# TensorE's loop of a four-layer kernel with two steps a turn: six turns in place of twelve

## The chip, the cores and the metric

The kernel runs on one core of one Trainium2 chip. The metric is the device time of one launch in microseconds. A core has five engines that run their own instruction streams and meet through semaphores: TensorE (PE, with its weight loads shown apart as PEld), VectorE (DVE), ScalarE (ACT), GpSimd (POOL), and SyncE (SP), which issues DMAs.

## The reference, cut to what matters

The input x is 64 sequences of 64 tokens with 512 features, float32. Four layers are applied, each added to its input:

```
x = x + x @ W.T + (x @ A[a].T) @ Bm[a].T * scal[a]   # layer 0, adapter a chosen for each sequence
x = x + w1[idx1].T @ x        # layer 1, 64x64 matrix over the tokens of each sequence
x = x + attention(x)          # layer 2, 16 heads of 32, causal, Wq, Wk, Wv, Wo
x = x + w3[idx3].T @ x        # layer 3, as layer 1 with another table
```

Large products are taken as three products of rounded parts (high by high, high by low, low by high), so one 128x128 block of a weight matrix costs three matmuls. The small products (scores, attention times values, layers 1 and 3, adapters) are float32 matmuls.

## The kernel before, in words

Four sequences (256 tokens) are worked on together and called a pair; there are 16 pairs (`PAIRS`). The kernel is a software pipeline in which step `i` works on several pairs at once: values, transposed probabilities and attention of pair `i`, layers 0 and 1 and keys, queries and scores of pair `i+1`, adapters of pair `i+2`, the output projection and layer 3 of pair `i-1`.

Each engine has its own `step(i)`, whose order is written out by hand, and all five run it through the same helper `in_steps` (L361). It writes out step 0, then a hardware loop (`Fori`) over steps 1 to `LAST_ALIKE` = 12, then writes out steps 13, 14 and 15. So each engine's program holds five copies of its step, of which one is the loop's body. Inside the loop `i` is a register, and a wait such as `pe.wait_ge(x1_copied, SEQT * i + 1)` compares with a value computed in a register; outside it `i` is a Python integer and the values are constants. The function `parted(i)` (L324) tells the two apart: in the steps written out, attention comes after query part 1, in the loop it comes after query part 3, directly ahead of the scores.

TensorE's step (L766 on) is, in order: `values` (L677, L679, L681), `layer0(i+1)` (L589, L591, L593) with the adapters, transposes of the probabilities (L702), `adapters_down` (L584), `layer1` (L633), `layer2_out(i-1)` (L748, L749, L755), more transposes, four `key_part`, four `query_part` (L649, L650, L654), with `layer3(i-1)` (L616) after query part 3, `attend` (L718) and last `scores(i+1)` (L694). `attend` and `scores` are 64 float32 matmuls each. The loop closes right after the scores, and the next turn begins with `values`. SP's step loads x, the chosen adapter rows and the layer 1 and 3 matrices ahead, and stores results. The other engines' steps follow the same order of pairs. Code ahead of TensorE's loop turns the weight matrices, computes the first pair, and runs step 0; code behind it runs three steps and the last layer.

Of the kernel before, what the change touches and what calls it, by code (L numbers as in the profile page):

```python
# [42 lines left out]
def cond_resid_kernel(nc, x, idx0, idx1, cond, idx3, W, A, Bm, scal, w1, Wq, Wk, Wv, Wo, w3, out):  # L43
# [12 lines left out]
    with ExitStack() as ctx:  # L56
# [262 lines left out]
        def after(i, n):  # L319

            return not isinstance(i, int) or 0 <= i + n < PAIRS


        def parted(i):  # L324
            return isinstance(i, int)
# [32 lines left out]

        LAST_ALIKE = PAIRS - 4

        def in_steps(engine, step):  # L361
            step(0)
            with engine.Fori(1, LAST_ALIKE + 1) as i:
                step(i)
            for i in range(LAST_ALIKE + 1, PAIRS):
                step(i)

# [135 lines left out]
        def _(pe):  # L503
# [68 lines left out]
            def adapters_down(i, x0_of=None):  # L572

                pe.wait_ge(a_ready, i)
                pe.wait_ge(x_turned, i)


                n = SEQT * RANK
                for c in range(NC):
                    for t in range(TILES):  # L580
                        if x0_of is not None and (c, t) == (NC - 1, TILES - 1):
                            layer1_ready(x0_of)
                        at = (c % 2 * TILES + t) * n
                        last = nc.tensor.matmul(bank[DOWN][at:at + n, 0:P], a_sel[:, c, t * n:(t + 1) * n],  # L584
                                                xT[:, c, tok(t)], start=(c < 2), stop=(c >= 2))
                last.then_inc(xa_mm, 1)
# [9 lines left out]
            def layer0(i):  # L596
                pe.wait_ge(xT_split, i)
                for t in range(TILES):
                    for c in range(NC):
                        layer0_part(t, c)  # L600
                    adapters_up(i, t)
# [17 lines left out]
            def layer1_ready(i):  # L619
                pe.wait_ge(w1_ready, i + 1)  # L620
                pe.wait_ge(x0_copied_act, i + 1)
                pe.wait_ge(x0_copied_dve, i + 1)
# [4 lines left out]
            def layer1():  # L627
                for t in range(TILES):
                    for h in range(S // SQ):
                        for r in range(SEQT):  # L630
                            for g in range(JG):
                                at = (2 * t + h) * P
                                last = nc.tensor.matmul(  # L633
                                    bank[MIX[r]][g * SQ:(g + 1) * SQ, at:at + P], w1_own[half(r), t, h * SQ:(h + 1) * SQ],
                                    x0[half(r), t, g * P:(g + 1) * P], start=True, stop=True)
                last.then_inc(x1_mm, 1)
# [21 lines left out]
            def key_part(i, m):  # L658
                last = project_T(WK, MIX, m, split=TILES * (i + 1) if m == 0 else None)
                if m % 2 == 1:  # L660
                    last.then_inc(k_mm, 1)

            def query_part(m, split=None):
                last = project_T(WQ, Q, m, split)
                if m % 2 == 1:
                    last.then_inc(q_mm, 1)

            def values(i, t, x0_of=None):
                if t == 1:
                    if after(i, -1):  # L670
                        pe.wait_ge(attn_split, SEQT * i)
                    else:
                        pe.wait_ge(xa_summed, 1)
                for c in range(NC):
                    if x0_of is not None and c == NC - 1:
                        layer1_ready(x0_of)
                    nc.tensor.matmul(bank[OUT[t]][:], x1T_hi[:, c, tok(t)], w_hi[:, WV, c, :],  # L677
                                     start=(c == 0), stop=False)
                    nc.tensor.matmul(bank[OUT[t]][:], x1T_hi[:, c, tok(t)], w_lo[:, WV, c, :],  # L679
                                     start=False, stop=False)  # L680
                    last = nc.tensor.matmul(bank[OUT[t]][:], x1T_lo[:, c, tok(t)], w_hi[:, WV, c, :],  # L681
                                            start=False, stop=(c == NC - 1))
                last.then_inc(v_mm, 1)
# [15 lines left out]
            def turn_probs(i, g, pieces):  # L699
                for at in pieces:  # L700
                    n, c = divmod(at, NC)
                    last = nc.tensor.transpose(bank[SC[2 * g + n]][:, c * P:(c + 1) * P],  # L702
                                               probs[:, g, at * P:(at + 1) * P], ident[:])
                    if at % NC == NC - 1:
                        last.then_inc(pT_mm, 1)
# [57 lines left out]
            def layer3(i):  # L763
                mix(x2, w3_own, y_banks(i), y_mm)

            def step(i):  # L766
                prev, nxt, nxt2 = after(i, -1), after(i, 1), after(i, 2)
                if not prev:
                    pe.wait_ge(part_split, len(PARTS_V))
                values(i, 0)  # L770
                if prev:
                    values(i, 1)
                if not nxt:
                    last_step(i)
                    return
                layer0(i + 1)
                if not prev:
                    values(i, 1, x0_of=i + 1)
                    layer1()
                pe.wait_ge(probs_done[0], i + 1)  # L780
                turn_probs(i, 0, range(7))
                turn_probs(i, 0, range(7, 8))
                if prev and not nxt2:
                    pe.wait_ge(probs_done[1], i + 1)
                    turn_probs(i, 1, range(7))
                    layer1_ready(i + 1)
                    turn_probs(i, 1, range(7, 8))
                if prev:
                    if nxt2:
                        pe.wait_ge(v_copied, TILES * (i + 1))  # L790
                        adapters_down(i + 2, x0_of=i + 1)
                    layer1()
                    for t in range(TILES):
                        layer2_out(i - 1, t)
                if nxt2:
                    pe.wait_ge(probs_done[1], i + 1)
                    turn_probs(i, 1, range(8))
                if not prev:
                    pe.wait_ge(v_copied, TILES)
                    adapters_down(2)  # L800
                pe.wait_ge(x1_hi_done, TILES * (i + 2))

                if not prev:
                    query_part(0, split=TILES * 2)
                pe.wait_ge(x1_copied, SEQT * i + 1)
                for m in range(NC):
                    if m == 2:
                        pe.wait_ge(x1_copied, SEQT * (i + 1))
                    key_part(i + 1, m)
                for m in range(NC) if prev else range(1, NC):  # L810
                    if m == 2:
                        pe.wait_ge(k_copied_act, i + 2)
                    if prev and m == (1 if parted(i) else 3):
                        pe.wait_ge(k_copied_dve, i + 2)
                        pT_copied(i, HG)
                        layer3_ready(i - 1)
                    query_part(m)
                    if m == (1 if parted(i) else 3):
                        if prev:
                            layer3(i - 1)  # L820
                        else:
                            pe.wait_ge(k_copied_dve, 2)
                            pT_copied(0, HG)
                            pe.wait_ge(xa_summed, 2)
                        attend()
                if prev:
                    pe.wait_ge(y_copied_act, i)
                    pe.wait_ge(y_copied_dve, i)
                else:
                    pe.wait_ge(part_split, len(PARTS_V) + len(PARTS_O))  # L830
                scores(i + 1)

            def last_step(i):
                for t in range(TILES):
                    layer2_out(i - 1, t)
                pe.wait_ge(probs_done[0], i + 1)
                turn_probs(i, 0, range(8))
                pe.wait_ge(probs_done[1], i + 1)
                turn_probs(i, 1, range(8))
                layer3_ready(i - 1)  # L840
                layer3(i - 1)
                pT_copied(i, HG)
                attend_last()
# [48 lines left out]
                query_part(m)  # L892
            adapters_down(1)
            scores(0)
            in_steps(pe, step)
            for t in range(TILES):
                layer2_out(PAIRS - 1, t)
            pe.wait_ge(w3_ready, PAIRS)
# [607 lines left out]
```

## Time and profile before

| what | value |
|---|---|
| median of 3 runs | 612.41 us (610.5 to 612.68) |
| the profiled execution, its own time | 612.43 us |
| span of its instructions | 610.6 us |
| TensorE busy | 602.3 us, 99% of the span |
| TensorE weight loads busy | 519.9 us, 85% |
| VectorE, ScalarE, GpSimd busy | 392.6, 224.6, 109.8 us |
| granted TensorE clock, mean | 0.997 |

The span runs from the first to the last instruction of the program; the device time is 1.8 us longer. Busy times are of the profiled execution. TensorE's weight loads run beside its matmuls and are recorded as instructions of their own. Register, semaphore and branch instructions are not counted as busy. Instruction packets are DMA packets that bring an engine's code; they stand in the DMA section under the kind "instruction".

### The profile page before, as it was taken

The numbers are of one execution on the slowest core, as the hardware profiler recorded it, in microseconds if no ns is written. First come the engines' busy times: TensorE is split into PE (matmuls) and PEld (weight loads), VectorE is DVE, ScalarE is ACT, GpSimd is POOL, SyncE is SP. The second block draws the span as 40 slices with busy tenths as digits, with TensorE's granted clock in tenths as the row PEclk, the third lists the DMA queues.
The fourth block names the chain that finished last, engine by engine and source line by source line (L and its number), as shares of the span: only waits on it lengthen the run. The fifth ranks groups of instructions, "written<-read, shape, count | busy, mean of one in ns | idle before, by whom it ended". The sixth has DMA issues, their size and how long they took to land.

```text
span 610.6 us, 21490 instructions
## 1 busy us (share of the span) xinstructions
PE 602.3 (99%) x8524; PEld 519.9 (85%) x8524; DVE 392.6 (64%) x573; ACT 224.6 (37%) x434; POOL 109.8 (18%) x101
## 2 busy tenths in 40 slices
PE   8999999899999999999999999999999999999998
PEld 8898889788898988889888898988889898888885
DVE  4799865665657566575765657567575766646374
ACT  4446342342424334251443424344251443513222
POOL 2013120301203030040402204040030302103030
PEclk9999999899999999999999999999999999999999
DMA  8962313222322322222231322322222231310212
GB/s 288 174 131 69 99 41 82 67 63 73 75 65 76 91 73 60 73 62 75 73 67 71 90 75 53 86 73 61 73 63 73 75 87 49 69 68 3 71 41 104
DMA packets 65273, 48.29 MB, mean 79 GB/s; under 512 B 16923, under 2 KB 51739, under 8 KB 65243
## 3 DMA queue, kind: packets, MB, share of 16 engines
q1 hardware_dynamic: 60090, 42.63, 26.8%
q10 hardware_dynamic: 5152, 5.24, 2.9%
q8 instruction: 21, 0.34, 0.2%
q14 instruction: 10, 0.07, 0.0%
HBM read 30.54 MB, written 17.30 MB: 78 GB/s over the span
## 4 chain that ended last, share of the span: by engine, by line
PE 97%; DVE 1%; DMA 1%; issue 1%; ACTq 0%; ACT 0%; DVEq 0%
PE banks L649 10%; PE banks L654 10%; PE banks L650 10%; PE banks L677 5%; PE banks L748 5%; PE banks L755 5%; PE banks L679 5%; PE banks L681 5%; PE banks L749 5%; PE banks L589 5%; PE banks L591 5%; PE banks L593 5%; PE banks L702 5%; PE banks L694 4%; PE banks L718 3%; PE banks L616 3%
## 5 line engine op out<-in xcount | busy, mean ns | idle before, releaser
L649 PE MATMUL banks<-x1T_hi,w_hi 128*128 128x256 f32 x512 | 129.8, 286 | 0.0
L650 PE MATMUL banks<-x1T_hi,w_lo 128*128 128x256 f32 x512 | 128.2, 283 | 0.0
L649 PEld LDWEIGHTS banks<-x1T_hi,w_hi 128*128 128x128 f32 x512 | 98.0, 191 | 0.7 <-ACT x1T_hi L914 0.4
L650 PEld LDWEIGHTS banks<-x1T_hi,w_lo 128*128 128x128 f32 x512 | 98.1, 192 | 0.0
L654 PE MATMUL banks<-x1T_lo,w_hi 128*128 128x256 f32 x512 | 82.4, 283 | 0.0
L1428 POOL TENSOR_TENSOR probs<-probs,row_max 128x1024 f32<-128x1024 f32 x32 | 61.0, 1906 | 112.5 <-DVE row_max L1209 112.5
L1410 POOL TENSOR_TENSOR w_own<-w_in,own 128x128 f32<-128x128 f32 x32 | 14.7, 460 | 364.6 <-PE banks L616 267.6
L654 PEld LDWEIGHTS banks<-x1T_lo,w_hi 128*128 128x128 f32 x512 | 70.6, 192 | 0.2 <-DVE x1T_lo L1120 0.2
L1195 DVE TENSOR_TENSOR qkT<-banks,beta 128x512 f32<-128x512 f32 x32 | 22.1, 690 | 59.4 <-PE banks L654 59.4
L914 ACT ACTIVATE x_y<-banks 128x512 f32<-128x512 f32 (+1 forms) x17 | 9.9, 585 | 128.8 <-PE banks L616 122.0
L1213 DVE TENSOR_REDUCE row_sum<-probs 128x16 f32<-128x1024 f32 x32 | 39.0, 1218 | 25.0 <-ACT probs L996 25.0
L677 PE MATMUL banks<-w_hi,x1T_hi 128*128 128x512 f32 x128 | 51.9, 405 | 1.3 <-issue 0.2
L748 PE MATMUL banks<-w_hi,attnT_hi 128*128 128x512 f32 x128 | 52.3, 409 | 0.0
L914 ACT ACTIVATE probsT<-banks 128x512 f32<-128x512 f32 x32 | 19.2, 598 | 85.9 <-PE banks L702 85.9
L681 PE MATMUL banks<-w_hi,x1T_lo 128*128 128x512 f32 x128 | 50.7, 396 | 0.0
L679 PE MATMUL banks<-w_lo,x1T_hi 128*128 128x512 f32 x128 | 50.7, 396 | 0.0
L589 PE MATMUL banks<-w_hi,xT_hi 128*128 128x512 f32 x128 | 50.4, 394 | 0.0
L749 PE MATMUL banks<-w_lo,attnT_hi 128*128 128x512 f32 x128 | 50.2, 392 | 0.0
L591 PE MATMUL banks<-w_lo,xT_hi 128*128 128x512 f32 x128 | 49.9, 390 | 0.0
L593 PE MATMUL banks<-w_hi,xT_lo 128*128 128x512 f32 x128 | 49.9, 390 | 0.0
L1230 DVE TENSOR_TENSOR x_y<-banks,x_kept 128x512 f32<-128x512 f32 x32 | 22.0, 691 | 37.7 <-PE banks L755 37.7
L996 ACT ACTIVATE probs<-probs 128x1024 f32<-128x1024 f32 x32 | 34.0, 1061 | 30.0 <-POOL probs L1428 30.0
(138 smaller groups left out, 1054.1 us busy)
## 6 DMA issues: line engine op xcount, KB each, us to landing
x_rows<-x_in SPq DMA_DIRECT2D x64, 128.0 KB, 2.4
x_kept<-x_rows SPq DMA_DIRECT2D x16, 512.0 KB, 3.6
x_in<-in_x_dram SPq DMA_DIRECT2D x60, 128.0 KB, 2.8
out_dram<-x_y SPq DMA_DIRECT2D x15, 512.0 KB, 3.0
b_sel<-b_parts SPq DMA_DIRECT2D x180, 32.0 KB, 1.7
w_in<-in_L_cond_weights_dram SPq DMA_DIRECT2D x128, 16.0 KB
probsT<-in_L_cond_W_dram ACTq DMA_DIRECT2D x1, 1024.0 KB, 6.1
probs<-in_L_cond_Wk_dram ACTq DMA_DIRECT2D x1, 1024.0 KB, 7.8
```

The source lines that it names most:

```text
L589: nc.tensor.matmul(bank[MIX[t]][:], xT_hi[:, c, tok(t)], w_hi[:, W0, c, :], start=(c == 0), stop=False)
L591: nc.tensor.matmul(bank[MIX[t]][:], xT_hi[:, c, tok(t)], w_lo[:, W0, c, :], start=False, stop=False)
L593: nc.tensor.matmul(bank[MIX[t]][:], xT_lo[:, c, tok(t)], w_hi[:, W0, c, :], start=False, stop=False)
L649: nc.tensor.matmul(out_ap, w_hi[:, w, c, cols], x1T_hi[:, c, :], start=(c == 0), stop=False)
L650: nc.tensor.matmul(out_ap, w_lo[:, w, c, cols], x1T_hi[:, c, :], start=False, stop=False)
L654: last = nc.tensor.matmul(out_ap, w_hi[:, w, c, cols], x1T_lo[:, c, :], start=False, stop=(c == NC - 1))
L677: nc.tensor.matmul(bank[OUT[t]][:], x1T_hi[:, c, tok(t)], w_hi[:, WV, c, :], start=(c == 0), stop=False)
L679: nc.tensor.matmul(bank[OUT[t]][:], x1T_hi[:, c, tok(t)], w_lo[:, WV, c, :], start=False, stop=False)
L681: last = nc.tensor.matmul(bank[OUT[t]][:], x1T_lo[:, c, tok(t)], w_hi[:, WV, c, :], start=False, stop=(c == NC - 1))
L748: nc.tensor.matmul(at[:], attnT_hi[:, c, tok(t)], w_hi[:, WO, c, :], start=(c == 0), stop=False)
L749: nc.tensor.matmul(at[:], attnT_hi[:, c, tok(t)], w_lo[:, WO, c, :], start=False, stop=False)
L1428: nc.gpsimd.tensor_tensor(heads(probs[:, g, :]), heads(probs[:, g, :]), rows[:, g, :].unsqueeze(2).to_broadcast([P, HEADS, S]), op).then_i ...
```

## The change

`in_steps` gets an argument for the number of steps that one turn of the loop holds, and TensorE alone calls it with 2. Its loop then runs from 1 to 12 in strides of two, and its body holds `step(i)` and `step(i + 1)`, both with registers. The other four engines keep one step a turn, and the steps written out (0, 13, 14, 15) stay as they are on every engine.

```diff
-        def in_steps(engine, step):
+        def in_steps(engine, step, steps_a_turn=1):
             step(0)
-            with engine.Fori(1, LAST_ALIKE + 1) as i:
-                step(i)
+            with engine.Fori(1, LAST_ALIKE + 1, steps_a_turn) as i:
+                for n in range(steps_a_turn):
+                    step(i + n if n else i)
             for i in range(LAST_ALIKE + 1, PAIRS):
                 step(i)
@@
-            in_steps(pe, step)
+            in_steps(pe, step, steps_a_turn=2)
```

## Rows read from the trace of the kernel before

**Rows 1.** The page: busy us (share) and instructions of each engine; the chain's shares.
```profile
PE 602.3 (99%) x8524; PEld 519.9 (85%) x8524; DVE 392.6 (64%) x573; ACT 224.6 (37%) x434; POOL 109.8 (18%) x101
...
PE 97%; DVE 1%; DMA 1%; issue 1%; ACTq 0%; ACT 0%; DVEq 0%
```

**Rows 2.** Waits of TensorE's matmuls, whole span: releaser, us in total, times, longest.
```profile
PE banks L694 <- issue: 1.6, 1, 1.6
PE banks L532 <- DVE still L1326: 1.1, 1, 1.1
...
PE banks L677 <- issue: 0.2, 1, 0.2
```

**Rows 3.** Source line L363, the loop: xcount, ns min/median/max, first and last start.
```profile
L363 PEldq COMPARE_BRANCH  x11: 76/208/213, 147.3 to 511.4; - x11
...
L363 PEldq MOVE  x10: 29/29/29, 147.5 to 475.2; - x10
```

**Rows 4.** Timeline of matmuls (start, us) at the loop's closing branch near 147.5.
```profile
145.90 1.59 PE L694 MATMUL banks<-qkT 32*64 32x64 f32 x128
147.61 0.47 PE L677 MATMUL banks<-w_hi,x1T_hi 128*128 128x512 f32 x1
```

**Rows 5.** The same near 511.5 and 548.2, where step follows step without a taken branch.
```profile
510.02 1.59 PE L694 MATMUL banks<-qkT 32*64 32x64 f32 x128
511.54 0.50 PE L677 MATMUL banks<-w_hi,x1T_hi 128*128 128x512 f32 x1
...
546.46 1.85 PE L694 MATMUL banks<-qkT 32*64 32x64 f32 x128
548.24 0.50 PE L677 MATMUL banks<-w_hi,x1T_hi 128*128 128x512 f32 x1
```

**Rows 6.** Windows (first three the whole span, last one turn): length, busy us (x), PEclk, DMA.
```profile
0.00:109.22 109.22, 105.28 (x1414) 92.98 (x1414) 79.52 (x126) 49.21 (x99) 17.76 (x33) 1.00 0.51 127
109.22:511.40 402.18, 400.83 (x5852) 346.60 (x5837) 256.12 (x363) 146.00 (x285) 73.00 (x55) 1.00 0.27 71
511.40:610.60 99.20, 96.17 (x1303) 80.31 (x1286) 56.95 (x86) 29.42 (x51) 18.99 (x13) 1.00 0.20 58
147.25:183.66 36.41, 36.29 (x553) 31.41 (x539) 23.34 (x35) 13.34 (x26) 6.63 (x5) 1.00 0.27 72
```

**Rows 7.** DMA queues of the whole span: packets, MB, share of 16 engines.
```profile
q8 instruction: 21, 0.34, 0.2%
```

**Rows 8.** All DMA queues of 112 to 512 us (columns as rows 7).
```profile
q1 hardware_dynamic: 41009, 28.81, 27.0%
```

**Rows 9.** DMA queues of 106.1 to 107.2 us, then instruction packets of 109.6 to 110.7 us.
```profile
q8 instruction: 1, 0.02, 5.8%
...
q8 instruction: 1, 0.02, 5.3%
```

**Rows 10.** Timeline of weight loads, end of the first turn (103 to 111 us).
```profile
104.49 1.32 PEld L718 LDWEIGHTS banks<-probsT,v 64*32 64x32 f32 x128 [0.81 <-issue]
105.90 0.89 PEld L694 LDWEIGHTS banks<-qkT 32*64 32x64 f32 x69
108.57 0.73 PEld L694 LDWEIGHTS banks<-qkT 32*64 32x64 f32 x59 [1.77 <-issue]
```

**Rows 11.** Timeline of weight loads, end of the second and the third turn.
```profile
144.48 1.32 PEld L718 LDWEIGHTS banks<-probsT,v 64*32 64x32 f32 x128 [0.81 <-issue]
...
180.90 1.31 PEld L718 LDWEIGHTS banks<-probsT,v 64*32 64x32 f32 x126
```

**Rows 12.** Chain in order of time, matmuls behind the first turn's branch.
```profile
111.73 0.43 PE banks L681
...
113.44 0.26 PE banks L677
113.70 0.23 PE banks L679
```

**Rows 13.** Windows of the same stretch, columns as rows 6.
```profile
104.00:107.00 3.00, 2.93 (x204) 2.21 (x197) 1.32 (x3) 1.59 (x3) 0.46 (x1) 1.00 0.16 60
...
109.60:113.40 3.80, 3.80 (x10) 2.98 (x11) 3.73 (x6) 0.26 (x1) 1.30 (x1) 0.55 0.10 21
113.40:117.00 3.60, 3.60 (x18) 2.95 (x17) 2.28 (x2) 1.60 (x3) 2.50 (x2) 1.00 0.52 146
```

## The prediction

> **What bounds the kernel now.** I read the page first. TensorE is busy 99% of the span and makes up 97% of the chain of work that ended last [rows 1], so what TensorE loses is lost by the kernel, and what the other engines wait for costs nothing. Next the waits: over the whole span the longest single wait of its matmuls is 1.6 us, put down to "issue", which means that nothing in the profile released it [rows 2]. The other waits there are at the start. So there is no stall on data for this change to touch. What it touches is the loop's own machinery: the branch, and where TensorE's instructions come from.
>
> **What the change removes.** Twelve turns close with one compare-and-branch each, of about 208 ns on the sequencer, and a register move at the head of the next turn [rows 3]. The cost on the engine is read off the matmuls. At the taken branch the last matmul of the scores ends at 145.90 + 1.59 = 147.49 and the first one of `values` starts at 147.61, 0.12 us later [rows 4]. Where step follows step with no taken branch, it starts before the last one's modelled end: 511.54 against 510.02 + 1.59 = 511.61, and 548.24 against 546.46 + 1.85 = 548.31, so -0.07 us both times [rows 5]. A taken branch therefore costs 0.12 + 0.07 = 0.19 us. Of the 11 taken branches 5 stay and 6 go: 6 x 0.19 = 1.1 us off. This is the whole gain that the branch itself can give. The register operations for the waits of `step(i + 1)` run on the sequencer ahead of the queue of matmuls. The same ones in today's body open no gap, since the matmuls of a whole turn are busy 36.29 of 36.41 us [rows 6], so I put them at 0. If that cover failed, a dozen operations a step at some 30 ns (the move) would be 0.4 us a step, 12 x 0.4 = 4.8 us at the most. The order of the work, the waits and all DMAs of the program stay the same, on every engine.
>
> **What the change adds: length of the body.** The trace has a queue, q8, that carries only instruction packets: 21 packets, 0.34 MB, thus 16 KB each [rows 7]. In the windows TensorE has 1414 + 1414 recorded instructions before the first closing branch, 1303 + 1286 after the last, and 553 + 539 in a turn's window [rows 6]. Some of those at the edges are counted in two windows. Its straight-line program is then the first window (which holds one turn) plus the last: 2828 + 2589 = 5417, and 21 packets for them is one for about 258. So q8 brings TensorE's code, some 260 instructions a packet. Of a turn's 1092 about 20 are counted twice, so a body is some 1070 engine instructions and about 20 of the sequencer, 4.2 packets. Between 112 and 512 us, eleven turns, q8 brings nothing at all [rows 8]: the body stays in the core and is run from there. A body of two steps is about 2160 instructions, 8.4 packets. Whether that stays too no row shows. The rows show that 4.2 packets and the one fetched beyond them [rows 9] stay. From below, the cost is nothing if it all stays. From above, each turn has to be fetched anew.
>
> What a fetched pass costs is shown once, because the first turn is one. Attend and scores are the fast stretch: 256 instructions each in 1.4 us [rows 10], against 36.4 us for the whole body. Only there does TensorE use up a packet faster than one is brought. In the first turn a packet lands in the window from 106.1 to 107.2 us, and it took 5.8% x 16 x 1.1 = 1.0 us [rows 9]. The weight loads stop in the middle of the scores at 106.8 and go on at 108.57, after 1.77 us of idle time, released by nothing [rows 10]. In every later turn the scores run through, as at 145.90 [rows 4]. This is the 1.6 us wait of rows 2. I read it as waiting for code. Behind it comes a second loss: from 109.6 to 113.4 the granted clock is 0.55, near the lower of its two levels (1.2 in place of 2.4 GHz), and before it TensorE had been idle in the scores [rows 10, 13]. A 512-column matmul takes 0.43 us there and 0.23 us after [rows 12]. Both losses together: from attend of the first turn to attend of the second it is 144.48 - 104.49 = 39.99 us, from there to the third 180.90 - 144.48 = 36.42 us [rows 10, 11]. One starved step costs 3.57 us.
>
> At a taken branch whose target is no longer in the core nothing is fetched ahead, so the whole time from need to use shows. Bounds: from below 0.19 us (today's branch), or 1.6 us, the wait in rows 2, if it is at all missed. From above: the packet of the first turn was asked for at the earliest when attend began, 104.49, and was in use at 108.57, 4.1 us. Nearer: it was in flight from about 106.1, and the boundary of the packet ahead of it lay 256 instructions before the stop, 106.8 - 1.4 = 105.4; 108.57 - 105.4 = 3.2 us. I take 3.2 us. A packet already in flight for the code behind the loop could add up to 2.5 us (106.1 to 108.57, the packet's start to its use).
>
> **The sum, for a body that doesn't stay.** In each of 12 loop steps attend and scores run through two packets within 2.9 us, so each starves once: 12 starved steps against 1 now, 11 x 3.57 = 39.3 us. Five taken branches miss: 5 x 3.2 = 16.0 us. Their slow clock falls together with that of the scores just before them, which is charged already; charging it twice would add 5 x 1.6 = 8 us. Branches removed: -1.1 us. Sum +54.2 us. Against the profiled execution's own time of 612.43 us, which is the median of the runs within 0.02 us, that makes 666.6, say 667 us. Nothing else covers this: all other engines wait for TensorE already. A starved step without the slow clock costs its 1.77 us and some 0.2 us of restart, which leaves 1.6 us of the 3.57 for the clock. The low end for the same mechanism: no slow clock, so 11 x (1.77 + 0.2) + 5 x 1.6 - 1.1 = 28.6, 641 us. The high end: 39.3 + 5 x (4.1 + 1.6 + 0.3) + 5 x 1.2 (half of a packet in flight) - 1.1 = 74, and with one more starved boundary in some turns about 80, 692 us.
>
> The Trainium skill bears on the one thing the rows leave open. "Runtime: NRT & Kernel Launch", section "Instruction fetch mechanics", says that an engine's instruction memory is filled in blocks of 16 KiB, 256 instructions, and that TensorE's holds 128 KiB, 2048 instructions. By that today's body fits and a body of some 2160 just does not. The packet size agrees with the trace (0.34 MB in 21); the capacity no row here shows.
>
> **The rivals.**
>
> A, the body stays in the core. Then there is only the gain: 612.4 - 1.1 = 611.3 us, not slower. For it: eleven turns without a packet [rows 8] show that the core keeps code well beyond the packet in use. Against it: nothing shown was larger than 5 or 6 packets, and this wants 9. It decides at a capacity of about 2160 instructions: above it A, below it the forecast. The skill's same section also speaks of a window of only two blocks, out of which a taken branch has to fetch. By that, today's loop would miss at each branch, and the trace disagrees: 0.19 us a branch and no packets in eleven turns. Were it true, halving the branches would save six misses.
>
> B, only the branches miss. The stop at 106.8 would be something that happens once, and code would otherwise be brought in time. Then 5 x (3.2 + 1.8) - 1.1 = +24, 636 us. For it: in steps 13 and 14, which run once, no such wait shows in rows 2. Against it: there attend doesn't stand before the scores but after query part 1, so no two packets are used up in a row; the one fetched pass with the loop's order did stop. Only a first turn with the same order is a fair comparison.
>
> C, a part of the body stays, and only the remainder is fetched each turn (a store that keeps the oldest code). Then one of two scores starves: some 5 x 3.57 + 5 x 1.6 = 26, 637 us.
>
> **How the numbers follow.** Forecast (refetched each turn) 0.77, A 0.14, B 0.04, C 0.03, and 0.02 for something that gains. What a measurement of this kernel can tell from no change is about 0.5%, 3 us. A's gain of 1.1 us lies within it, so A is "same", and "faster" has 0.02; 0.84 are slower. The predicted time is 667 us. The range runs from 636, which takes in B and C and the case without slow clock, to 692. It leaves out A.
>
> **What would show it.** Right: q8 carries 9 or 10 packets in each of six turns, some 70 to 78 in all in place of 21; weight loads of L694 show a wait on issue of about 1.8 us in every loop step; at five places L677 starts 3 us or more after the scores; the granted clock falls in about every loop step, and its mean to near 0.95; a turn of two steps takes about 83 us (72.8 + 2 x 3.57 + 3.2) where two turns took 72.8; VectorE, ScalarE and GpSimd are as busy as before in us. Wrong: 21 packets and L694 without waits mean A. Packets in each turn but waits at L677 alone mean B. If packets and waits are as said and the clock stays up, the time is near 641 us and the term of the clock was wrong.

## The result and the profile after

The changed kernel takes 667.15 us (median of 4 runs, 661.65 to 669.08) against 611.88 us for the kernel before in the same runs: 8.9% slower, ratio 1.0891, 95% interval 1.0822 to 1.0960. The profiled execution took 666.39 us.

The page of the changed kernel (its lines are numbered one higher, so L694 is now L695 and L677 is L678), to be laid beside [rows 1] and [rows 7]:

```profile
span 664.6 us, 21442 instructions
...
PE 615.9 (93%) x8524; PEld 529.4 (80%) x8524; DVE 393.7 (59%) x573; ACT 224.5 (34%) x434; POOL 109.7 (17%) x101
...
q8 instruction: 75, 1.23, 0.8%
...
PE 91%; issue 7%; DVE 1%; ACT 0%; DVEq 0%
```

The same 8524 matmuls ran. The queue that brings TensorE's code carried 75 packets in place of 21, and "issue" went from 1% to 7% of the chain. The waits of its matmuls (releaser, us in total, times, longest), beside [rows 2]:

```profile
PE banks L678 <- issue: 22.7, 5, 4.8
PE banks L695 <- issue: 21.3, 12, 2.2
PE banks L533 <- DVE still L1327: 1.1, 1, 1.1
```

Twelve waits in the scores, one in each loop step, where there was one; and five at the first matmul behind a taken branch. The span grew by 664.6 - 610.6 = 54.0 us. The two kinds of wait grew by 21.3 - 1.6 and 22.7 - 0.2, together 42.2 us, and TensorE's busy time by 615.9 - 602.3 = 13.6 us, which is mostly the same matmuls at a slower clock. The sum is 55.8 us, 1.8 more than the span grew; the branches that went account for about 1 us of that, the rest is not explained (matmul ends are modelled).

The source line of the loop, beside [rows 3]: six closing branches, and those that are taken last 4.5 us on the sequencer in place of 0.2.

```profile
L363 PEldq COMPARE_BRANCH  x6: 79/4552/4848, 148.2 to 565.4; - x6
```

The end of the first turn, weight loads in order of time (start, us, count, idle before), beside [rows 10]:

```profile
143.25 1.32 PEld L719 LDWEIGHTS banks<-probsT,v 64*32 64x32 f32 x128 [0.81 <-issue]
144.66 0.61 PEld L695 LDWEIGHTS banks<-qkT 32*64 32x64 f32 x44
147.27 1.02 PEld L695 LDWEIGHTS banks<-qkT 32*64 32x64 f32 x84 [2.00 <-issue]
153.12 0.29 PEld L678 LDWEIGHTS banks<-w_hi,x1T_hi 128*128 128x128 f32 x1 [4.83 <-issue]
```

The scores stop after 44 of 128 weight loads, since the body's blocks now fall elsewhere in the second step, and behind the branch nothing runs for 4.83 us. The instruction packets of 112 to 565 us (where [rows 8] show none over most of the same work), of 148 to 152 us, the branch alone, and of 153 to 155.5 us:

```profile
q8 instruction: 53, 0.87, 0.9%
...
q8 instruction: 2, 0.03, 6.4%
...
q8 instruction: 1, 0.02, 3.3%
```

Two packets are in flight during the wait at the branch, not one. Windows of three turns, of the matmuls right behind the first branch, and of those after (length, busy us of PE, PEld, DVE, ACT, POOL, granted clock, DMA share and GB/s), beside [rows 6, 13]:

```profile
148.20:231.20 83.00, 74.77 (x1074) 64.27 (x1067) 46.86 (x66) 26.64 (x52) 13.26 (x10) 0.96 0.25 65
231.20:315.50 84.30, 76.23 (x1083) 65.39 (x1073) 46.87 (x66) 26.46 (x53) 13.26 (x10) 0.94 0.24 64
315.50:398.40 82.90, 74.83 (x1074) 64.31 (x1065) 46.87 (x66) 26.50 (x52) 13.27 (x10) 0.96 0.24 65
153.10:160.00 6.90, 6.85 (x23) 5.55 (x24) 0.95 (x2) 1.55 (x2) 1.90 (x1) 0.74 0.30 81
160.00:166.00 6.00, 6.00 (x28) 4.97 (x27) 3.58 (x5) 2.14 (x3) 1.90 (x1) 1.00 0.00 0
```

A turn of two steps takes 83 to 84 us, against 2 x 36.41 = 72.8. VectorE, ScalarE and GpSimd are as busy as in two turns before. Behind the branch the clock is at its lower level (1.2 GHz) until about 156.5, after the stop in the scores, their short products and the idle time at the branch. The chain shows it matmul by matmul, as [rows 12] did:

```profile
148.43 4.72 issue
153.15 0.77 PE banks L678
...
156.04 0.43 PE banks L678
156.47 0.39 PE banks L680
156.86 0.24 PE banks L682
```

### The profile page after: what moved, and what is told of

The parts are those of the page before. It is cut to its first block, busy times and chain, and to the rows that moved or that the text cites. A ratio compares the mean times of both kernels' runs of the same rounds, so it can differ in the third digit from the quotient of the medians.

```text
span 664.6 us, 21442 instructions
## 1 busy us (share of the span) xinstructions
PE 615.9 (93%) x8524; PEld 529.4 (80%) x8524; DVE 393.7 (59%) x573; ACT 224.5 (34%) x434; POOL 109.7 (17%) x101
## 4 chain that ended last, share of the span: by engine, by line
PE 91%; issue 7%; DVE 1%; ACT 0%; DVEq 0%
PE banks L650 9%; PE banks L655 9%; PE banks L651 9%; PE banks L678 6%; PE banks L680 5%; PE banks L749 5%; PE banks L682 5%; PE banks L756 4%; PE banks L750 4%; PE banks L590 4%; PE banks L592 4%; PE banks L594 4%; PE banks L703 4%; PE banks L695 4%; PE banks L719 3%
## 5 line engine op out<-in xcount | busy, mean ns | idle before, releaser
L1429 POOL TENSOR_TENSOR probs<-probs,row_max 128x1024 f32<-128x1024 f32 x32 | 60.9, 1904 | 133.6 <-DVE row_max L1210 133.6
L678 PE MATMUL banks<-w_hi,x1T_hi 128*128 128x512 f32 x128 | 56.6, 442 | 22.7 <-issue 22.7
L1205 DVE TENSOR_TENSOR probs<-banks,mask 128x512 f32<-128x512 f32 x64 | 41.1, 684 | 23.5 <-PE banks L695 23.4
L680 PE MATMUL banks<-w_lo,x1T_hi 128*128 128x512 f32 x128 | 54.5, 426 | 0.0
L682 PE MATMUL banks<-w_hi,x1T_lo 128*128 128x512 f32 x128 | 53.6, 419 | 0.0
L915 ACT ACTIVATE v<-banks 128x512 f32<-128x512 f32 x32 | 19.2, 599 | 94.6 <-PE banks L682 94.1
L678 PEld LDWEIGHTS banks<-w_hi,x1T_hi 128*128 128x128 f32 x128 | 26.8, 209 | 29.6 <-issue 23.2
L695 PE MATMUL banks<-qkT 32*64 32x64 f32 x2048 | 29.7, 232 | 21.9 <-issue 21.3
```

The costliest lines, as they stand in the source:

```text
L695: last = nc.tensor.matmul(bank[SC[j]][half(h), key_columns(m, t, r)], qT[rows, m, own_tokens(t, r)], kT[rows, m, own_tokens(t, r)], start= ...
L1429: nc.gpsimd.tensor_tensor(heads(probs[:, g, :]), heads(probs[:, g, :]), rows[:, g, :].unsqueeze(2).to_broadcast([P, HEADS, S]), op).then_i ...
```

## The experiments

All times are medians beside runs of the kernel before on the same chip (medians 610.98 to 612.29 us); the changed kernel's 667.15 us was timed beside 611.88. The theory: a body of two steps doesn't stay in the core, so each pass is fetched; the engine waits where two blocks of code are used up within the time that one takes to come, and at each taken branch, whose target is gone.

**Is it the number of branches or the length of the body?** `three` takes three steps a turn, `unrolled` writes out all sixteen on TensorE in the loop's own order.

```diff
-            in_steps(pe, step, steps_a_turn=2)
+            in_steps(pe, step, steps_a_turn=3)
```
```diff
-            return isinstance(i, int)
+            return isinstance(i, int) and not 1 <= i <= PAIRS - 4
@@
-            in_steps(pe, step, steps_a_turn=2)
+            for i in range(PAIRS):
+                step(i)
```

> Three steps a turn, four turns. Theory (cost goes by fetched passes and by taken branches): twelve waits in the scores as with two steps, but only three branches that miss: 667 less 2 x (4.6 wait + about 3 of slow clock) = 650 to 653 us; q8 carries about 70 packets. Rival (the cost grows with the length of the body): at or above 667 us, with longer waits at the branch.

> TensorE's sixteen steps all written out, no loop, with the loop's own order in steps 1 to 12. Theory: no branch, so no wait at L678 and no 6.8 us slow clock, but twelve fetched passes: twelve waits in the scores of about 1.9 us. 612.4 - 3.6 - 2.1 + 12 x 1.95 + a third of 12 x 1.6 = 636 us; q8 carries about 67 packets. Rival (the loss in the scores belongs to the body of two steps, not to fetched code): no waits, 610 us.

Measured: `three` 651.95 us (ratio 1.0663, 1.0626 to 1.0699), `unrolled` 634.77 us (1.0388, 1.0366 to 1.0410), with 71 and 67 packets. Waits of the matmuls in `three`, then in `unrolled`:

```profile
PE banks L695 <- issue: 16.4, 12, 1.8
PE banks L678 <- issue: 12.7, 3, 4.3
```
```profile
PE banks L695 <- issue: 17.9, 11, 2.2
PE banks L678 <- issue: 2.4, 1, 2.4
```

The longer body is the cheaper one, because fewer branches miss. Without any branch twelve waits stay, one of which falls just behind the scores. So the five misses are worth (667.15 - 634.77) / 5 = 6.5 us each by the one comparison and (667.15 - 651.95) / 2 = 7.6 us by the other, of which the wait is 4.5 us. The time of the changed kernel is uncertain by some 4 us, so these two are one value within their noise. Both times met the expectation.

**Is it two blocks in a row?** In `apart2` attention goes back to after query part 1 in the loop too, as in the steps written out. `apart1` is the same with one step a turn, `unrolled_apart` the same with no loop.

```diff
         def parted(i):
-            return isinstance(i, int)
+            return True
```

> Two steps a turn with attention after query part 1 in the loop. Theory (waits in the scores come of two packets used up in a row): the twelve waits at L695 vanish though q8 still carries about 75 packets; the five at L678 stay, perhaps shorter. Time 667 - 12 x 1.95 - 2 x 1.6 = 640 us. Rival (each fetch costs the engine something wherever it falls): waits of 1 us or more move to other lines and the time stays above 655 us.

> One step a turn, as before the change, but in the loop too attention comes after query part 1 and so no longer directly ahead of the scores (TensorE's order and VectorE's with it, as in the steps written out). Theory (the wait of 1.77 us in the first turn is a starved fetch, because attend and scores use up two packets in under 3 us): that wait and the slow clock behind it vanish, 3.6 us less: 608.8 us, unless the order costs something of its own in the loop. Rival (the wait belongs to something that happens once at that time): it stays, and 612.4 us.

> TensorE's sixteen steps written out, with attention after query part 1 in all. Theory: all code is fetched, but never two packets in a row, and there is no branch: neither kind of wait. 612.4 - 3.6 - 11 x 0.19 = 606.7 us, faster than both kernels. Rival (fetching costs even when it is ahead): between 612 and 640 us.

Measured: `apart2` 640.47 us (1.0472, 1.0450 to 1.0493), `apart1` 613.20 us (1.0025, 1.0015 to 1.0034), `unrolled_apart` 614.01 us (1.0039, 1.0024 to 1.0054). The queue line and the waits of `apart2`:

```profile
q8 instruction: 75, 1.23, 0.9%
...
PE banks L678 <- issue: 20.1, 5, 4.2
PE banks L533 <- DVE still L1327: 1.1, 1, 1.1
```

As many packets as in the changed kernel, and not one wait on issue in the scores; the time was as expected. Fetching as such costs little: `unrolled_apart` brings 67 packets and is 0.8 us slower than `apart1` with 21, though it is also spared eleven taken branches, so that 46 more packets cost some 2 us, of which 0.9 us stands as waits on issue. In `apart1` the 1.6 us wait of [rows 2] is gone as well. The order itself costs something, which I had not allowed for. By its closing branches a turn takes (512.3 - 144.7) / 10 = 36.76 us, where the order before takes (511.4 - 147.3) / 10 = 36.41 [rows 3]:

```profile
L363 PEldq COMPARE_BRANCH  x11: 76/208/212, 144.7 to 512.3; - x11
```

Twelve times 0.35 is 4.2 us, which more than takes back the 3.6 us of the first turn. That is why both of these came out above the kernel before, where I had expected them below it. What in that order costs 0.35 us was not followed up.

The 3.6 us of the first turn consist of two parts that come apart. The stretch of slow clock behind its wait ([rows 13]; 3.5 us at half the clock are the 0.003 that the mean granted clock of 0.997 is short of 1) is not there in every execution. Of the 44 executions of the kernel before beside which the experiments were timed, 21 had a mean granted clock of 0.997 and a median of 612.50 us, and 22 had 1.000 and 610.94 us. So that slow clock costs 1.6 us and came behind the same wait about every second time (read from the mean clock of each execution; only one of them has a trace here). `apart1`, nearly always at 1.000, is 2.3 us slower than the second group, which is the order's 4.2 us less the 1.97 us of the wait.

**How much stays?** Two kernels of two steps with smaller bodies. `half_attend2` leaves out half of the attention products in the loop steps, about 1904 instructions; `half_both2` half of the scores too, about 1648.

```diff
-            def attend():
-                for t in range(TILES):
+            def attend(i):
+                for t in range(TILES) if parted(i) else range(1):
@@ scores, in half_both2 alone
-                    for t in range(TILES):
+                    for t in range(TILES) if parted(i) else range(1):
```

> Two steps a turn, with half of the attention products left out in the loop steps (the output is wrong in these rows), which takes 128 instructions out of each step: a body of about 1904 instructions, 7.4 packets, which with its offset touches 8 blocks. What comes out at two capacities: if the store simply holds 2048 instructions, the loop stays in the core from the second turn on: some 21 packets plus a few, no waits at L678, about 612 - 12 x 0.7 - 1 = 603 us. If one of eight blocks is always given to the block fetched ahead, the head is lost all the same: 60 packets or more, five waits of over 3 us at L678, and a time above 630 us. I hold the second for likelier (0.6).

> Two steps a turn, with half of the attention products and half of the score products left out in the loop steps (wrong output): a body of about 1648 instructions, 6.4 packets, which touches 7 blocks. Theory (a store of some 2048 instructions): it stays in the core from the second turn on, q8 carries under 30 packets, one fetched turn, no wait above 1 us at L678, time about 612 - 12 x 1.4 - 1 = 594 us plus at most 4. Rival (any body of two steps pays at its branch, whatever its size): five waits of 3 us or more at L678 and a time near 594 + 50.

Measured: `half_attend2` 649.68 us, `half_both2` 596.40 us, one run each. Packets and longest waits of `half_attend2`, then of `half_both2`:

```profile
q8 instruction: 69, 1.13, 0.9%
...
PE banks L678 <- issue: 24.7, 5, 5.2
PE banks L680 <- issue: 8.9, 6, 1.7
```
```profile
q8 instruction: 23, 0.38, 0.3%
...
PE banks L695 <- issue: 2.7, 11, 0.2
PE banks L533 <- DVE still L1327: 1.1, 1, 1.1
```

Two steps a turn are harmless where the body is small enough: 23 packets, no wait at the branch. And 1904 instructions, below the 2048 that the Trainium skill gives for TensorE ("Runtime: NRT & Kernel Launch", "Instruction fetch mechanics"), are too many. This fits a store of eight blocks in which one is taken by the block fetched ahead of use: 1904 instructions beginning at slot 67 touch eight blocks, 1648 touch seven. That is a reading of two points. The runs show only that the limit lies between 1648 and 1904 instructions for this offset.

`half_attend2` shows one more thing: its six waits at L680. They stand a few instructions behind the scores, in the first step of each turn. Weight loads of the first turn:

```profile
104.89 0.70 PEld L719 LDWEIGHTS banks<-probsT,v 64*32 64x32 f32 x64 [0.81 <-issue]
106.00 1.46 PEld L695 LDWEIGHTS banks<-qkT 32*64 32x64 f32 x128 [0.41 <-issue]
...
110.39 0.19 PEld L682 LDWEIGHTS banks<-w_hi,x1T_lo 128*128 128x128 f32 x1 [1.87 <-issue]
```

Only 2 x (64 + 128) = 384 short instructions (weight loads and matmuls) follow each other there, not two blocks' worth, and the packet that ends the wait starts at 108.1. I read from it that one block of 256 is enough, if it is used up in about 1.5 us while the next takes, by the prediction's estimate, over 3 us from the entry of the block before it. With 256 in a row, in the order of `apart2`, the longest such wait was 0.6 us (`unrolled_apart`, whose blocks end at another place in each step).

**What is the branch itself worth?** With bodies that stay, one step against two.

```diff
-            in_steps(pe, step, steps_a_turn=2)
+            in_steps(pe, step, steps_a_turn=1)
```

> One step a turn, with the same half of the attention and of the score products left out in the loop steps as in half_both2 (wrong output). With its twin it measures the branch term by itself, where the body stays in the core with one and with two steps. It keeps eleven taken branches where the twin has five: at 0.19 us each it should be 1.1 us slower than the twin. If the branch costs nothing, or the second step's register work takes as much as it saves, there is no difference.

> half_both2 again, two steps a turn with the same halves left out, timed beside its twin of one step a turn: 1.1 us faster than that, about 595 to 596.5 us, 21 to 24 instruction packets on q8.

Measured: `half_both1` 597.20 us (596.93 to 597.24, 5 runs), `half_both2_again` 596.43 us (596.13 to 596.50, 5 runs). Six branches fewer give 0.77 us, 0.13 us each, against my 0.19. This is net of any register work that the second step adds.

**Can the branch be told in time?** In `hint2` TensorE's loop names its closing branch's target at the head of each turn; `hint_apart2` adds the order of `apart2`.

```diff
-            with engine.Fori(1, LAST_ALIKE + 1, steps_a_turn) as i:
+            with (nc.Fori(1, LAST_ALIKE + 1, steps_a_turn, engines=[mybir.EngineType.PE], hint_back_edge=True)
+                  if steps_a_turn > 1 else engine.Fori(1, LAST_ALIKE + 1)) as i:
```

> Two steps a turn as in the change, but TensorE's loop names the target of its closing branch at the head of each turn, so that its code can be fetched ahead of the branch. Theory (the code at the head is no longer in the core when the branch is taken): the five waits at L678, 22.7 us in the changed kernel, fall below 5 us in all, the slow-clock stretches of 6.8 us behind them shrink to 3.4 us or vanish, the twelve waits in the scores stay near 1.9 us each. Time 667 - 18 - 5 x 2 to 3 = 635 to 640 us. Rival (a branch over a longer body, or the flush of the queue, costs that much by itself): the waits at L678 stay above 4 us each and the time at 667 us.

> Two steps a turn, attention after query part 1, and the closing branch's target named at the head of each turn. From the two single runs: no waits in the scores, five waits at L678 of 3.2 - 1 = 2 to 3 us in place of 4.2 (naming the target took 1.5 us off each where attend stood ahead of the scores, because it is fetched only once the last block is entered, 180 instructions ahead of the branch). Time 640.5 - 5 x 1.4 = 633 us, 630 if the slow clock shortens with them.

Measured: `hint2` 660.96 us (1.0790, 1.0748 to 1.0831), `hint_apart2` 630.87 us (1.0321, 1.0296 to 1.0347). Queue and waits of `hint2`, then of `hint_apart2`:

```profile
q8 instruction: 71, 1.16, 0.8%
...
PE banks L696 <- issue: 23.3, 12, 2.3
PE banks L679 <- issue: 15.5, 5, 3.2
```
```profile
q8 instruction: 71, 1.16, 0.8%
...
PE banks L679 <- issue: 11.5, 5, 2.4
```

My first expectation was a miss: I thought the target's code would be there, and the five waits fell only from 4.5 to 3.1 us each. The slow clock behind them stayed too (mean granted clock 0.972). The second expectation was met. Four packets fewer fit the reading that naming the target spares the fetch of the useless block behind the loop, but that the right one is still asked for only once the last block is entered, some 180 instructions and 1 us ahead of the branch. The packets' times bear it out. In the changed kernel one packet starts at 148.4 us, at the branch itself, and a second at 149.2. In `hint2` the last block is entered when the scores go on at 147.72, and between 148 and 152 us, which takes in the whole wait at the branch, one packet starts, at 148.8:

```profile
q8 instruction: 1, 0.02, 2.2%
```

All five waits at the branch hold two packets in the changed kernel and one in `hint2`. In `hint_apart2` the wait is shorter, 2.3 us; why was not followed up.

**Does the place of a boundary matter?** `placed1` is the kernel before, one step a turn in its own order, with the head of TensorE's loop put at slot 197 of a block of 256.

```diff
-            with engine.Fori(1, LAST_ALIKE + 1) as i:
+            with (nc.Fori(1, LAST_ALIKE + 1, engines=[mybir.EngineType.PE], head_slot={mybir.EngineType.PE: 197})
+                  if engine is nc.tensor else engine.Fori(1, LAST_ALIKE + 1)) as i:
```

> The kernel before, one step a turn, with the loop's first instruction put at slot 197 of a block of 256 (it stands at about 67 now). The blocks' boundaries then fall a few instructions into attend and a few into the scores, so that the 0.81 us in which TensorE waits ahead of attend lies between the first one's fetch and the second one's need, and the third comes after the branch. Theory (the wait in the first turn is the time from one boundary to the next short of some 3.2 us): the wait of 1.77 us shrinks to about 1 us and moves to the start of the scores, the slow clock behind it may go: 610 to 612 us. If the place of a boundary doesn't matter: 1.77 us in the scores and 612.2 us.

Measured: 609.06 us (608.68 to 609.24) against 612.29, ratio 0.9956 (0.9941 to 0.9970): 0.4% below the kernel before, the fastest of the kernels that leave nothing out. Its first turn, with the same 21 packets, to be laid beside [rows 10]; then the instruction packets of 100 to 103 us and of 105 to 107 us:

```profile
104.56 1.32 PEld L720 LDWEIGHTS banks<-probsT,v 64*32 64x32 f32 x128 [0.81 <-issue]
105.97 1.46 PEld L696 LDWEIGHTS banks<-qkT 32*64 32x64 f32 x128
107.69 0.19 PEld L679 LDWEIGHTS banks<-w_hi,x1T_hi 128*128 128x128 f32 x1 [0.26 <-issue]
```
```profile
q8 instruction: 1, 0.02, 2.8%
...
q8 instruction: 1, 0.02, 4.2%
```

The wait did not shrink to 1 us, it is gone, and the slow clock with it. Against the executions of the kernel before in which the slow clock was absent as well (610.73 us) that leaves 1.7 us, which is the wait by itself. The first of these packets starts at 102.6 us, during the queries, the second at 106.8. The second can't be the scores' block, since the scores run from 105.97 on without a stop; so that block was brought by the first, asked for over 3 us before the scores began and before attend began at 104.56. I had expected it to be asked for in attend. In the kernel before, no packet came between 100 and 106 us, and the one for the second part of the scores started at 106.1, 0.7 us before it was needed.

## Why the prediction was right

**The step that decided it** was that a body of 8.4 packets doesn't stay. It held: 75 packets (70 to 78 predicted), and with `half_both2`, where the body stays, the whole loss is absent. Rival A fell with it, and B too, since twelve waits in the scores appeared. C, that a part of the body stays, doesn't fit twelve waits, nor 53 packets between 112 and 565 us, which is about 4.2 for each of eleven steps and one more at each taken branch.

**The time** was 667 us predicted, 667.15 measured. That close a hit is luck: the four executions lie between 661.65 and 669.08 us, and the two large terms were each off in opposite directions. The mechanism was right, their sizes were not.

- The starved steps were put at 11 x 3.57 = 39.3 us. The waits were as said, 21.3 - 1.6 = 19.7 us for eleven. But I charged each with a slow clock, as in the one example I had, and even there it came only every second time; the runs of the kernel before, 610.5 to 612.68 us, held both cases. The granted clock fell behind all five taken branches. Of the twelve waits in the scores five stand just ahead of those; behind the seven others the clock fell only twice, and behind two of the twelve waits of `unrolled`, whose mean granted clock is 0.995. The length of the stop doesn't decide it: of two waits of 1.6 us in the changed kernel, at 190.5 and at 272.9 us, only the second was followed by a slow clock (windows below). By `unrolled` against `unrolled_apart`, with the order's 4.2 us added, (634.77 - 614.01 + 4.2) / 12 = 2.1 us a step. The term should have been about 23 us, 16 less.
- The missed branches were put at 5 x 3.2 = 16.0 us, with no slow clock of their own. They cost 6.5 to 7.6 us each, 33 to 38 us: 4.5 us of waiting and about 2 or more of slow clock. My reason for leaving the clock out, that it is charged with the stop in the scores just before, moved five of the eleven clock charges to the wrong term. The wait was 1.3 us longer than my 3.2. About half of the 2.5 us for a packet in flight, which I had kept for the high end, belonged in the value: two packets show in each such wait, and naming the target took 1.4 us off.
- Sorted the other way, the forecast held 11 x 1.97 + 16.0 = 37.7 us of waiting and 11 x 1.6 = 17.6 us of slow clock; measured were 42.2 us of waiting and 13.6 us of added busy time. The waiting was put 4.5 us too low, the clock 4.0 us too high.
- The branches removed were put at 1.1 us and gave 0.77 us where they could be seen alone. The register work of the second step was rightly put near nothing: if six branches are worth 1.1 us, it took at most the 0.4 us that are missing.

The windows behind the two waits, columns as rows 6; the third number from the end is the granted clock:

```profile
190.00:198.00 8.00, 6.38 (x118) 5.29 (x116) 6.19 (x8) 2.73 (x8) 1.91 (x1) 1.00 0.24 82
273.00:281.00 8.00, 6.51 (x78) 5.26 (x78) 5.77 (x8) 2.09 (x7) 2.43 (x2) 0.79 0.23 73
```

**The signs** named for the forecast: a turn of 83 us (83.0, 84.3, 82.9), waits of 1.8 us in the scores in each loop step, five waits over 3 us at L678, other engines as busy as before, all held. "The granted clock falls in about every loop step" didn't, and its mean was 0.969 in place of 0.95.

## What to carry to other kernels

Before a loop's body is made longer to save branches, count its instructions on the engine against what that engine keeps. Here the saving was 0.13 us a branch and the loss 4.5 us or more a turn on top of one wait a step, and in this kernel it was harmless at 1648 instructions and no longer at 1904. An instruction queue that is silent during a loop says that the body stays; a wait on "issue" in the first turn alone says about how long a fetched pass would wait, while the slow clock seen behind it once need not come again. Where code must be fetched, or in a first turn, keep runs of short instructions to a block's worth: 256 in a row cost at most 0.6 us here, 384 cost up to 1.7. Or place the loop's head so that the boundaries fall outside them.

## What the runs showed of the hardware that was not expected

- A fetched pass costs TensorE next to nothing where long instructions part the short ones: 67 packets over 612 us in `unrolled_apart`, with waits on issue of 0.9 us in all.
- Three steps a turn are faster than two by 15.2 us, because two taken branches fewer miss; the waits in the scores stay twelve.
- In the wait at a missed branch two packets are in flight: 4.5 us behind attend and scores, 4.0 us behind scores alone (`apart2`). With the target named it is one packet: 3.1 and 2.3 us.
- In this kernel a stop of 2 us in the scores seldom lowered the granted clock, while each stop of 4 us at the branch did, in the changed kernel, `three` and `apart2`. In `hint_apart2` stops of 2.2 to 2.4 us at the branch were followed by a slow clock four times of five.
- The slow clock behind the first turn's wait comes in about half of the executions of the kernel before, and splits its times into 610.94 and 612.50 us.
- With the loop's head at another slot of its block the wait of the first turn is gone, at the same number of packets: 609.06 us.
